# An expert layer on one core: GpSimd's loop written out tile by tile, its indirect DMAs fed from the table's own columns

## What is computed

```python
logits = xt @ router_w + router_b
scores = softmax(logits) + router_bias
# best 2 of 4 groups of experts, then the best 2 experts among those
vals = take_along_axis(scores, idx, axis=1)
gate = zeros((T, E)).at[arange(T)[:, None], idx].add(vals)
for each expert e of 16:                      # T = 2048, E = 16
    h = silu(xt @ w1 + b1) * (xt @ w2 + b2)   # 512 -> 128
    y = y + gate[:, e, None] * (h @ w3 + b3)  # 128 -> 512
z = (silu(xt @ sw1 + sb1) * (xt @ sw2 + sb2)) @ sw3 + sb3   # 512 -> 256 -> 512
return x + y + z
```

## Time and profile before

| | |
|---|---|
| median of 3 runs | 282.46 us (282.38, 282.46, 290.04) |
| profiled execution, span | 282.6 us |
| PE busy | 253.3 us (90%) |
| DVE busy | 150.1 us (53%) |
| ACT busy | 78.6 us (28%) |
| POOL busy | 126.0 us (45%) |
| mean granted TensorE clock | 0.988 |

### The profile page before, as it was taken

The page is one execution under the profiler, slowest core; times in us unless marked ns, Lnnn a source line. Parts: engine busy times, 40 slices in busy tenths (PEclk is TensorE's granted clock), DMA queues, the critical chain, the costliest instruction groups (busy, mean ns, idle before and its releaser), DMA issues.

```text
span 282.6 us, 4281 instructions
## 1 busy us (share of the span) xinstructions
PE 253.3 (90%) x1092; PEld 163.0 (58%) x1093; DVE 150.1 (53%) x314; ACT 78.6 (28%) x169; POOL 126.0 (45%) x204
## 2 busy tenths in 40 slices
PE   7959889899999859999999889889988979999975
PEld 6826667688864436677775455545555544444421
DVE  0497988569799763344333322332233130179894
ACT  2213455303164002333433232223322221000400
POOL 7673445310111456565656556565656565000160
PEclk9977999999999999999999999999999999999999
DMA  7996876882639359533443343434344433799963
GB/s 224 328 402 217 296 249 205 319 328 121 223 113 420 137 157 369 178 116 119 141 133 121 117 112 107 124 103 148 111 119 140 139 124 118 241 390 388 395 255 148
DMA packets 20699, 57.91 MB, mean 205 GB/s; under 512 B 2533, under 2 KB 2533, under 8 KB 20428
## 3 DMA queue, kind: packets, MB, share of 16 engines
q1 hardware_dynamic: 15084, 39.89, 39.2%
q0 software_dynamic: 5600, 17.83, 19.7%
HBM read 40.94 MB, written 17.30 MB: 206 GB/s over the span
## 4 chain that ended last, share of the span: by engine, by line
PE 38%; issue 26%; POOL 18%; DVE 12%; POOLq 3%; DMA 2%; ACT 0%
PE psum L560 36%; POOL late_region L486 12%; DVE r L959 3%; POOL from_slot L483 3%; DVE xT L1189 2%; POOL to_slot L493 2%; DVE xT L954 2%; DVE xT L928 2%; PE psum L603 2%; DVE xT L969 1%; POOL expert_rows L497 1%; DMA late_region<-xt_rows,from_slot 1%; DMA xT<-cond_pack 1%; DVE mix_bias L956 1%; POOLq L480 1%
## 5 line engine op out<-in xcount | busy, mean ns | idle before, releaser
L560 PE MATMUL psum<-wexp,r 128*128 x272 | 70.2, 387 | 2.1 <-issue 1.2
L560 PEld LDWEIGHTS psum<-wexp,r 128*128 128x128 f32 x272 | 47.1, 190 | 28.9 <-issue 22.8
L928 DVE TENSOR_TENSOR r<-psum,ebias 128x256 f32<-128x256 f32 x34 | 14.4, 425 | 82.5 <-PE psum L560 82.5
L486 POOL DMA_INDIRECT late_region<-xt_rows,from_slot x36 | 36.7, 1019 | 28.5 <-POOL from_slot L483 25.3
L497 POOL DMA_INDIRECT expert_rows<-late_region,to_slot x34 | 34.0, 1001 | 30.1 <-POOL to_slot L493 28.3
L560 PE MATMUL psum<-wexp,xt_sb 128*128 x68 | 36.7, 621 | 7.9 <-issue 7.9
L560 PE MATMUL psum<-xT,shared_sb 128*128 128x512 f32 x64 | 28.0, 593 | 0.8 <-issue 0.8
L871 ACT ACTIVATE late_region<-psum 128x512 f32<-128x512 f32 x34 | 20.3, 597 | 29.5 <-PE psum L560 29.5
L865 ACT ACTIVATE r<-r 128x128 f32<-128x128 f32 x34 | 10.5, 309 | 60.2 <-DVE r L928 60.2
L706 PE MATMUL psum<-ident,late_region 128*128 128x128 f32 x144 | 22.3, 277 | 3.6 <-DMA late_region<-xt_rows,from_slot 3.5
L1145 DVE COPY r<-psum 128x512 f32<-128x512 f32 x36 | 24.6, 684 | 1.5 <-PE psum L706 1.3
(11 more groups left out here) (175 smaller groups left out, 327.7 us busy)
## 6 DMA issues: line engine op xcount, KB each, us to landing
wexp<-expert_pack SPq DMA_DIRECT2D x16, 768.0 KB, 5.2
wexp<-expert_rows SPq DMA_DIRECT2D x8, 1024.0 KB, 13.0
xt_rows<-xt_sb SPq DMA_DIRECT2D x16, 256.0 KB, 2.5
x_early<-x SPq DMA_DIRECT2D x2, 1024.0 KB, 9.0
late_region<-x SPq DMA_DIRECT2D x2, 1024.0 KB, 13.7
ebias<-expert_bias SPq DMA_DIRECT2D x1, 2048.0 KB, 7.2
out_dram<-x_early SPq DMA_DIRECT2D x8, 256.0 KB, 9.8
shared_sb<-shared_pack SPq DMA_DIRECT2D x1, 1536.0 KB, 16.7
```

The lines of the kernel that those rows point to most:

```text
L486: nc.gpsimd.indirect_dma_start(out=xg[:, slot, :], out_offset=None, in_=xt_dram[:, :], in_offset=bass.IndirectOffsetOnAxis(ap=from_slot[:, ...
L560: return nc.tensor.matmul(dst, lhsT, rhs, start=start, stop=stop)
L928: return nc.vector.tensor_tensor(dst, a, b, op)
```

## The change

It is all on POOL.

- The `Fori` is gone: all pairs up to `SURE - 2` are written out by a Python loop, and so are the pairs under `If`s, up to `PAIRS`. Tile numbers are constants.
- The gathers and scatters take their indices from column i of `from_row` and `to_row`. The copies, `from_slot`, the semaphore `from_copied` and the waits for copies are gone, except for the last tile, whose number is known at run time only: its column is copied to `to_slot`, now one column wide.
- `hold` and its semaphore `pool_held` are gone: a wait is a plain `wait_ge`.
- The wait for the counts and their loads into registers come after 14 written-out pairs, not after four gathers.
- The pairs that may not exist are nested differently: seven `If`s, one after another, stand between the last pair and the last scatter when there are 17 pairs.

```diff
-        to_slot = sb("to_slot", [P, RING], I32)
-        from_slot = sb("from_slot", [P, RING], I32)
+        to_slot = sb("to_slot", [P, 1], I32)
...
-            def gather(i, slot):
-                nc.gpsimd.tensor_copy(from_slot[:, slot:slot + 1], from_row[:, bass.ds(i, 1)]
-                                      ).then_inc(from_copied, 1)
-                hold(from_copied, i + 1)
+            def gather(i):
                 nc.gpsimd.indirect_dma_start(
-                    out=xg[:, slot, :], out_offset=None, in_=xt_dram[:, :],
-                    in_offset=bass.IndirectOffsetOnAxis(ap=from_slot[:, slot:slot + 1].bitcast(U32), axis=0),
-                ).then_inc(xg_loaded[slot], 16)
-
-            def scatter(i, slot):
-                hold(y_ready, i + 1)
-                nc.gpsimd.tensor_copy(to_slot[:, slot:slot + 1], to_row[:, bass.ds(i, 1)]
-                                      ).then_inc(to_copied, 1)
-                hold(to_copied, i + 1)
+                    out=xg[:, i % RING, :], out_offset=None, in_=xt_dram[:, :],
+                    in_offset=bass.IndirectOffsetOnAxis(ap=from_row[:, i:i + 1].bitcast(U32), axis=0),
+                ).then_inc(xg_loaded[i % RING], 16)
+
+            def gather_ahead(i):
+                pool.wait_ge(xgT_done, i - RING + 1)
+                gather(i)
+
+            def scatter(rows, slot):
                 nc.gpsimd.indirect_dma_start(
-                    out=y_dram[:, :],
-                    out_offset=bass.IndirectOffsetOnAxis(ap=to_slot[:, slot:slot + 1].bitcast(U32), axis=0),
+                    out=y_dram[:, :], out_offset=bass.IndirectOffsetOnAxis(ap=rows.bitcast(U32), axis=0),
                     in_=y_sb[:, slot, :], in_offset=None, bounds_check=ASSIGN - 1, oob_is_err=False,
                 ).then_inc(scattered[slot], 16)
...
+            def scatter_tile(i):
+                pool.wait_ge(y_ready, i + 1)
+                scatter(to_row[:, i:i + 1], i % RING)
+
+            def pool_pair(p):
+                for i in (2 * p, 2 * p + 1):
+                    gather_ahead(i + AHEAD)
+                    if i >= 1:
+                        scatter_tile(i - 1)
+
+            def closing_pair(p):
+                with pool.If(pairs > p + 2):
+                    pool_pair(p)
+                with pool.If(pairs < p + 3):
+                    scatter_tile(2 * p - 1)
+                    scatter_tile(2 * p)
 
             for i in range(RING):
-                gather(i, i)
+                gather(i)
+            for i in range(RING, AHEAD):
+                gather_ahead(i)
+            for p in range(SURE - 2):
+                pool_pair(p)
             pool.wait_ge(counts_ready, 1)
             pairs, tiles = count_of(pool, N_PAIRS), count_of(pool, N_TILES)
...
-            with pool.Fori(1, (SURE - 2) // 2) as j:
-                for q in range(2):
-                    pool_pair(j * 2 + q, q)
...
-            scatter(tiles - 1, 1)
+            closing_pair(SURE - 2)
+            closing_pair(SURE - 1)
+            for p in range(SURE, PAIRS):
+                with pool.If(pairs > p):
+                    closing_pair(p)
+            pool.wait_ge(y_ready, tiles)
+            nc.gpsimd.tensor_copy(to_slot[:, :], to_row[:, bass.ds(tiles - 1, 1)]).then_inc(to_copied, 1)
+            pool.wait_ge(to_copied, 1)
+            scatter(to_slot[:, :], 1)
```

More of the change, by code:

```diff
@@ L50, in adaln_moe_ffn @@
     RING = 4
+    AHEAD = 6
     x_rows = x.rearrange("b c d -> (b c) d")
@@ L252, in adaln_moe_ffn @@
         z_ready = sem("z_ready")
-        from_copied = sem("from_copied")
         to_copied = sem("to_copied")
-        pool_held = sem("pool_held")
         xg_loaded = [sem(f"xg_loaded{r}") for r in range(RING)]
@@ L475, in _ @@
             pool.wait_ge(tables_ready, 1)
-            def hold(semaphore, value):
-                pool.wait_ge(semaphore, value)
-                pool.sem_inc(pool_held, 1)
-            def gather(i, slot):
-                nc.gpsimd.tensor_copy(from_slot[:, slot:slot + 1], from_row[:, bass.ds(i, 1)]
-                                      ).then_inc(from_copied, 1)
-                hold(from_copied, i + 1)
-                nc.gpsimd.indirect_dma_start(
-                    out=xg[:, slot, :], out_offset=None, in_=xt_dram[:, :],
-                    in_offset=bass.IndirectOffsetOnAxis(ap=from_slot[:, slot:slot + 1].bitcast(U32), axis=0),
-                ).then_inc(xg_loaded[slot], 16)
@@ L501, in scatter @@
                 ).then_inc(scattered[slot], 16)
[L505 to L515, removed]
-            for i in range(RING):
-                gather(i, i)
+            def scatter_tile(i):
+                pool.wait_ge(y_ready, i + 1)
+                scatter(to_row[:, i:i + 1], i % RING)
@@ L529, in closing_pair @@
[L529 to L546, removed]
```

## The result

The changed kernel takes 261.19 us in the median, against 282.42 us for the kernel before on the same chip: a ratio of 0.922, interval 0.914 to 0.930. It was run once more on a second chip, beside the kernel before.

A forecast was written before the change was run, and what follows sets the result against it. The prediction took POOL's queue, at 4.06 us a step against PE's 3.136, to bound the loop. Its terms summed as 282.6 - 18.7 - 1.0 - 1.5 + 0.5 = 261.9, stated as 262 us, range 259.5 to 270.

The forecast's parts named there:

- The main term: Loop, step 12 to 33: going at PE's 3.136 us a step instead of 84.57 us in all saves 18.7 us.
- Inside POOL's period: POOL's 4.06 us step: the DMA's 0.52 us hand-over lies bare only because it must wait for its copy.
- fourth rival: POOL's queue: plain waits stop it as `hold` did, or copies weren't the cause; pair near 4 us, 281 us; chance 0.04.
- Copies and waits removed: POOL's step: without both copies the DMA pair takes 2.0 to 2.4 us, bounded by 2.00 and 3.65, under PE's 3.136.
- first rival: POOL stays the loop's bound: two indirect DMAs still cost 3.58 to 3.65 us; 267.8 to 269.7 us; chance 0.14.
- The start: First gathers: the first tile comes about 0.4 us earlier, the second 1.2 or more; 1.0 us saved.
- The way out of the loops: Steps 31 to 33: PE's change of code, covered by POOL before, may now show; 0.5 us charged.
- The end of the loop: Step 33 to the shared expert: PE's queue, no longer at a gather's semaphore, loads ahead; 1.5 us saved, 0.8 to 1.6 possible.
- The skipped blocks: Seven blocks before the last scatter: branches cost some 0.5 us, covered by POOL's 3.1 us of waiting, so nothing.
- second rival: Written-out code costs instruction fetches: two of 2.8 us in the seven blocks exceed the cover by 2.5; 264.5 us; chance 0.06.
- third rival: Straight part of POOL's code: fetches add over 1.7 us a step, so the kernel ends slower than before; chance 0.02.

The follow-up runs named there:

- The spare copies: Kernel after the change plus one, four or eight unawaited 128x1 copies ahead of each gather and scatter of the first 28 steps: 260.40, 263.79, 290.05 us.
- the halves: Kernel after the change, but with a waited copy for the scatters only (262.57 us, 0.927) or for the gathers only (260.89 us, 0.926).
- e1: Kernel after the change, but each gather and scatter again copies its column and waits for it with a plain wait: 266.11 us, ratio 0.942.
- e11: e1 plus a bounds check on the gathers, which puts a register MOVE ahead of each gather's DMA: 284.26 us, ratio 1.004.
- e10: e1 plus a semaphore increment by POOL's queue after each wait for a copy: 283.83 us, ratio 1.005.
- e9: Kernel after the change, but the last scatter is written out too and reads the table directly, without its copy: 263.28 us, ratio 0.926.

## Why the prediction was right, and where its reasons weren't

**The bound and the size.** That the loop went at POOL's 4.06 us and would go at PE's 3.136 was right: it goes at 3.130. The main term, 18.7 us from step 12 to 33, measured 84.57 - 65.74 = 18.8. The spare copies and the halves bear out that PE's pace is the floor and POOL's step decides above it. That the step fits in PE's even with each hand-over bare, with 0.6 us to spare, was right too: `hold` without copies leaves 0.53.

**Inside POOL's period.** Here the reason failed, in the sentence that the 0.52 us "lies bare only because the DMA can't be handed over until its copy is done". A DMA can be handed over while its wait is open, if the wait is on the DMA. With that reason I expected 281 us of e1 and got 266. The gather's hand-over was bared by `hold`'s increment, the scatter's by the increment and, without it, by the MOVE. The prediction's fourth rival held that plain waits might stop the queue as `hold` did: they don't where a DMA follows directly (0.27 against 0.79), and they do where a MOVE stands between (0.81). The total didn't suffer, since the change takes away both copies and `hold`.

The Trainium skill, page Perfetto Trace Analysis, section DMA Instruction — SWDGE (GPSIMD), describes this: such a DMA is pushed into a wait queue, where the semaphore is waited for while the sequencer goes on. e1 and e11 agree with it (0.27 and 0.77 us).

**Copies and waits removed.** I took 2.0 to 2.4 us for the pair; it is 2.6, since 0.30 us stay between two DMAs. That is within the bounds of 2.00 to 3.65, and below 3.13, so nothing came of it. POOL-bound at 269 (first rival) would have needed 0.79 between them.

The rule of the Trainium skill's page Perfetto Trace Analysis, section GPSIMD Engine Instruction, that one should go by the spacing of starts is the right way to read it: 1.25 us a DMA, not the 0.95 of its span. But the spacing without a copy is far from the 1.79 that I drew from the rule.

**The start** was mis-sized: 1.0 us taken, up to 1.3 allowed, 2.2 measured. From the table (95.31 before, 94.33 after, DVE's write of `from_row`) to step 0's bias it was 12.13 us and is 9.96. What was mis-sized is the first tile, taken at 0.4: from the table to PE's first transposes it was 5.79 us (to 101.10) and is 4.16 (to 98.49), 1.6 less. The first gather begins 0.50 us after DVE starts to write the table, where it was 1.38, and is shorter, 1.20 against 1.94; why it is shorter, no run shows. All in all the start came 1.2 us sooner than I had taken.

**The way out of the loops** was charged with 0.5 and costs nothing: steps 31 to 33 follow at 3.13 and 3.14 us. **The end of the loop** gave 1.69, 1.5 taken. The time from the shared expert's first matmuls to the end is 49.7 before and 49.6 after.

**The sum by profiles.** 18.8 + 2.2 + 1.7 and 0.1 (the tail) is 22.8, and 1.0 more lies before the table, where nothing was changed; together the 23.8 between the two spans. By medians it is 21.2. The execution profiled before is some 2.1 us longer than its median, the one after 0.5 shorter; in which stretch, no row shows. My 20.7 was 2.1 short of the terms' 22.8 on the profiles. That it came within 0.5 of the medians is partly luck: the terms were 2.1 too small, and the 1.9 us around the span, which I had put at nothing, were left out. With both put right the sum is 282.6 - 22.8 + 1.9 = 261.7, nearly the same number.

**The skipped blocks** (second rival) cost nothing. The branches after:

```profile
L519 POOLq COMPARE_BRANCH  x8: 40/45/50, 204.1 to 211.3; - x8
```

The last is at 211.3, and ACT's last result at 213.62 (213.02 + 0.60). The last scatter comes 5.56 us after the shared expert starts, not over 6. The Trainium skill's rule of a fetch on a far branch (Runtime: NRT & Kernel Launch, Instruction fetch mechanics) shows nowhere in these rows. Nor does the written-out code show in the time: e10 and e11, written out, are at 1.005 and 1.004 of before, so neither a gain from the loop's removal nor a loss from fetches can be told (third rival).

What stays open is why e9 has 0.5 us more outside its span, and how much of its loss is the overlap of the adds and how much the clock.

## What to carry to other kernels

Read the bound by stretches and by periods: an engine at 45% busy can set the pace, and what a faster queue gives is read from the next engine's own pace, here 3.13 us a step. When a queue must wait, let the wait sit on the instruction that needs it: with a queue-handled instruction between wait and DMA (a counter increment, a register move) the hand-over of 0.52 us comes after the wait, for every DMA. Before a rewrite, look for the cheaper half: plain waits and one of the two tables read directly would have given nearly all of it (0.926 and 0.927 against 0.922 and 0.919).

## What the runs showed of the hardware

A plain wait between a copy and the indirect DMA that needs it costs 0.27 us of idle on GpSimd, with a MOVE or a semaphore increment of the queue in between 0.77 to 0.89. Two indirect DMAs back to back start 1.25 us apart, 1.50 and 1.38 for the first two pairs. Copies of a 128x1 column cost 0.20 us alone and 0.13 each in a row of four or eight (0.55 for four, 1.00 to 1.08 for eight). And the last 20 matmuls of the kernel follow a pause of PE, 2.08 us in the profile after and 2.09 in another execution of the same kernel, with a clock of 1.00 before it in both. In the first they took 7.98 us of busy time at a granted clock of 1.00, in the second 9.67 us at 0.83: for a part of the stretch PE was at the lower of its clock's two levels (1.2 and 2.4 GHz). That is one source of the 1 to 2 us between executions. Busy time by engine in that stretch, first of the profile after:

```profile
247.60:256.00 8.40, 7.98 (x20) 3.34 (x20) 6.65 (x11) 0.00 (x0) 1.59 (x2) 1.00 0.58 217
```

and then of the same kernel on the second chip:

```profile
246.90:256.70 9.80, 9.67 (x20) 3.90 (x20) 6.45 (x11) 0.00 (x0) 1.58 (x2) 0.83 0.47 175
```
